# A graph attention kernel: bound of |t| from the norm of the attention vector, transposes on two banks, ten weight halves split inside the attention loop

## What is computed

```python
h = relu(layernorm(x))
HW = h @ W
s, t = HW @ a[:512], HW @ a[512:]
e = leaky_relu(s[row] + t[col], 0.2)
att = softmax of e over the edges of each row
agg = segment_sum(att * h[col], row)
x = x + silu(agg) @ base_w.T + einsum('nip,oip->no', b_splines(agg), spline_w)
h = relu(layernorm(x))
x = x + three graph convolutions of h with batch norm and relu
```

## Time and profile before

| | us |
|---|---|
| median of 3 runs | 684.33 (682.5 to 684.81) |
| the profiled execution | 683.7 |
| its span in the trace | 681.9 |
| TensorE matmuls busy | 604.3 |
| VectorE busy | 477.9 |
| ScalarE busy | 371.5 |
| mean granted TensorE clock | 0.95 of 2.4 GHz |

### The profile page before, as it was taken

The page is one execution under the profiler, slowest core; times in us unless marked ns, Lnnn a source line. Parts: engine busy times, 40 slices in busy tenths (PEclk is TensorE's granted clock), DMA queues, the critical chain, the costliest instruction groups (busy, mean ns, idle before and its releaser), DMA issues.

```text
span 681.9 us, 8727 instructions
## 1 busy us (share of the span) xinstructions
PE 604.3 (89%) x3437; PEld 428.2 (63%) x3437; DVE 477.9 (70%) x739; ACT 371.5 (54%) x486; POOL 23.3 (3%) x30
## 2 busy tenths in 40 slices
PE   3766655999968999999999999869999999999994
PEld 2535643555534455555555555448999899988994
DVE  7989698999785999997369865784344434542354
ACT  1798597545779998987198620328331422332111
POOL 2000000000000000000000000202300020000000
PEclk9798686999979899999999999979999999999998
DMA  8553400000040000000001000090100000001202
GB/s 278 192 186 126 195 1 0 1 1 1 0 151 0 2 1 0 1 1 1 1 1 62 1 0 1 23 369 15 62 1 1 0 1 1 1 0 56 94 38 113
DMA packets 11417, 33.73 MB, mean 49 GB/s; under 512 B 718, under 2 KB 1038, under 8 KB 11120
## 3 DMA queue, kind: packets, MB, share of 16 engines
q1 hardware_dynamic: 11376, 33.17, 13.8%
HBM read 24.78 MB, written 8.40 MB: 49 GB/s over the span
## 4 chain that ended last, share of the span: by engine, by line
PE 67%; DVE 18%; ACT 8%; issue 4%; DVEq 1%; ACTq 1%; DMA 0%; SPq 0%
PE bank L1482 32%; PE bank L1557 20%; PE bank L1526 12%; DVE AL L994 2%; DVE OR L847 2%; DVE OM L850 2%; DVE EX L987 1%; DVE EX L999 1%; DVE SCR L958 1%; ACT CT L599 1%; PE bank L1328 1%; ACT JSQ L532 1%; ACT WKh L606 1%; DVE RDN L1029 1%; DVE hL L1004 1%
## 5 line engine op out<-in xcount | busy, mean ns | idle before, releaser
L1482 PE MATMUL bank<-BHL,WKh 128*128 128x418 f16 x1152 | 207.1, 342 | 4.2 <-DVE BHL L1083 4.2
L1482 PEld LDWEIGHTS bank<-BHL,WKh 128*128 128x128 f16 x1152 | 112.0, 97 | 99.3 <-DVE BHL L1083 4.6
L1557 PE MATMUL bank<-CF,YL 128*128 128x418 f32 x360 | 127.5, 354 | 0.0
L1557 PE MATMUL bank<-CF,YH 128*128 128x418 f32 x360 | 126.6, 352 | 0.0
L1277 DVE TENSOR_TENSOR Z<-bank,dvb 128x418 f32<-128x418 f32 x36 | 21.3, 593 | 69.1 <-PE bank L1557 69.1
L1557 PEld LDWEIGHTS bank<-CF,YL 128*128 128x128 f32 x360 | 67.6, 188 | 1.8
L1557 PEld LDWEIGHTS bank<-CF,YH 128*128 128x128 f32 x360 | 67.7, 188 | 1.0
L784 ACT ACTIVATE bnc<-bnm,tiny 128x1 f32<-128x1 f32 x12 | 3.5, 294 | 104.9 <-DVE bnm L1283 104.9
L1335 PE MATMUL bank<-OM,OR 128*128 128x160 f16 x320 | 32.3, 268 | 19.7 <-DVE OM L850 13.7
L1228 DVE SCALAR_TENSOR_TENSOR YL<-bank,dvc,YH 128x512 fp32r<-128x512 f32 x30 | 21.9, 748 | 38.5 <-ACT YH L765 38.5
L1526 PE MATMUL bank<-GWH,XH 128*128 128x512 f32 x120 | 48.1, 401 | 0.0
(11 more groups left out here) (202 smaller groups left out, 1010.6 us busy)
## 6 DMA issues: line engine op xcount, KB each, us to landing
WKf<-in_wk SPq DMA_DIRECT2D x9, 1024.0 KB, 5.4
c_scratch<-C SPq DMA_DIRECT2D x1, 3200.0 KB, 10.9
GWf<-in_gwT SPq DMA_DIRECT2D x3, 1024.0 KB, 5.4
C<-c_scratch SPq DMA_DIRECT2D x1, 2880.0 KB, 10.4
XT<-in_xT SPq DMA_DIRECT2D x1, 2500.0 KB, 8.8
x_scratch<-XT SPq DMA_DIRECT2D x1, 2500.0 KB, 16.1
XR<-x_scratch SPq DMA_DIRECT2D x1, 2500.0 KB, 8.9
outT<-Z SPq DMA_DIRECT2D x4, 625.0 KB, 3.1
```

The source lines that it names most:

```text
L1482: ins = mm(bank[:, 4 * (g % 2) + o, 0:G], lhs, rhs, start=(u == 0 and q == 0 and i == 0), stop=(u == UNITS - 1 and q == PAIR - 1 and i == 2))
L1557: ins = mm(bank[:, YB + u % YB, 0:G], Y[:, j, o * P:(o + 1) * P], CF[:, j, g * G:(g + 1) * G], start=(j == 0 and i == 0), stop=(j == NT - ...
```

## The change

- ScalarE no longer copies the spread vectors to WAB; VectorE reads them in banks 6 and 7. ScalarE instead takes the squared norm of the vector for t, and from it the bound of |t| (Square and Sqrt, at group 12 of the counts).
- The bound is added to the column of t before TensorE spreads it. The masks' maxima read the spread row in its banks. The reduction for max|t| and the tile U go. Six mask tiles take the place of two, and the scratch of the maxima is f16 in two buffers.
- TensorE transposes tile 0, spreads t, forms the degrees, and then transposes tiles 1 to 9, now with two banks for all. ScalarE does sums of squares 3 and 4 behind tile 0, and 5 to 8 in steps 1, 3, 5 and 7 of the loop. The Exp table is loaded ahead of the first row copies.
- The banks of the attention's sums are dealt out anew, with the denominator last in the first seven tiles. The scale of the weights is formed at step 13, and the second group waits for it.
- The first ten weight halves are split in steps 16 to 25 of the loop: the high half behind the rounding copy of the step on ScalarE, the low half at the end of the step on VectorE. The stretch behind the loop no longer has them.
- Masks and low halves of h are on VectorE, as before.

```diff
+LATE_SQUARES = (1, 3, 5, 7)
 LASTS = 3
+MASKS = 6
+BOUND = 1.02
+FIRST_HALF = 16
...
-        U = at("U", Z4 + 7680, [NP], F32)
-        SCR = at("SCR", Z4 + 8960, [NP], F32)
-        MSK = at("MSK", Z4 + 10240, [2, NP], F16)
-        WAB = at("WAB", Z4 + 12800, [2, D], F32)
+        MSK = at("MSK", Z4 + 5120, [MASKS, NP], F16)
+        JHs = [at("JH0", Z4 + 8960, [NT, D], F16), at("JH1", Z4 + 2560, [NT, D], F16)]
+        SCR = at("SCR", Z4 + 8960, [2, NP], F16)
...
+        def low_weights(g):
+
+            return AL0 if g == 0 else AL12[:, g - 1, :, :]
+
+        def att_bank(g, k):
+
+            return (3, 4, 0)[g] if k == 0 else 4 * ((g + 1) % 2) + k - 1
...
                 if n == 12:
                     act.wait_ge(wa_spread, 1)
-                    nc.scalar.copy(WAB[:, :, :], bank[:, 6:8, :]).then_inc(wa_set, 1)
+                    nc.scalar.activation(JST[:, 0, :], bank[:, 7, :], ACT.Square, accum_out=tb[:, 0:1])
+                    act.drain()
+                    nc.scalar.activation(tb[:, 1:2], tb[:, 0:1], ACT.Sqrt, bias=tiny[:, 0:1], scale=BOUND * D
+                                         ).then_inc(t_bound, 1)
...
-                    nc.scalar.copy(CT[:, t, 5 * b * P:5 * (b + 1) * P], bank16[:, 4 + 2 * (t % 2) + b, 0:5 * P]
+                    nc.scalar.copy(CT[:, t, 5 * b * P:5 * (b + 1) * P], bank16[:, 4 + b, 0:5 * P]
                                    ).then_inc(tposed_out, 1)
 
-            for t in range(5):
-                transposed(t)
+            transposed(0)
+            sum_squares(3, JSQ)
+            sum_squares(4, JSQ)
             act.wait_ge(degs_done, 1)
             nc.scalar.activation(dvc[:, :], bank[:, 3, 0:NT], ACT.Sqrt, bias=1.0).then_inc(degs_out, 1)
-            act.wait_ge(t_spread, 1)
-            act.wait_ge(t_scale, 1)
-            nc.scalar.activation(U[:, :], bank[:, 0:3, :].rearrange("p b c -> p (b c)")[:, 0:NP], ACT.Identity,
-                                 bias=tb[:, 1:2]).then_inc(t_used, 1)
-            for t in range(5, NT):
+            act.wait_ge(squares, 5)
+            for t in range(1, NT):
...
-            sum_squares(3, JSQ2)
-            sum_squares(4, JSQ2)
+            nc.scalar.activation(mv[:, 0, 0:1], tiny[:, 0:1], ACT.Exp)
+            attention_rows(0)
             act.wait_ge(dv_spread, 1)
-            nc.scalar.copy(dvb[:, :], bank[:, 0:3, :].rearrange("p b c -> p (b c)")[:, 0:NP]).then_inc(dvb_set, 1)
-            attention_rows(0)
-            sum_squares(5, JSQ2)
-            sum_squares(6, JSQ2)
+            nc.scalar.copy(dvb[:, :], bank[:, 3:6, :].rearrange("p b c -> p (b c)")[:, 0:NP]).then_inc(dvb_set, 1)
             attention_rows(1)
-            sum_squares(7, JSQ2)
-            sum_squares(8, JSQ2)
-            nc.scalar.activation(mv[:, 0, 0:1], tiny[:, 0:1], ACT.Exp)
-            attention_rows(2)
 
             def exponentials(n):
...
+            def weights_high(u):
+                act.wait_ge(wscale_set, 1)
+                act.wait_ge(agg_unit, DC + 1)
+                if u >= 2:
+                    act.wait_ge(wk_low, u - 1)
+                nc.scalar.mul(weights(u)[:, 0, :], raw_weights(u), wsc[:, 0:1]).then_inc(wk_high, 1)
+
             exponentials(0)
+            attention_rows(2)
             for n in range(NG * NT):
                 g, j = divmod(n, NT)
                 if n + 1 < NG * NT:
                     exponentials(n + 1)
                 act.wait_ge(att_f32, n + 1)
                 nc.scalar.copy(CT[:, j, g * G:(g + 1) * G], EX[:, n % 3, :]).then_inc(att_high, 1)
-
-            def weights_high(u):
-                act.wait_ge(wscale_set, 1)
-                act.wait_ge(att_low, NG * NT)
-                if u >= 2:
-                    act.wait_ge(wk_low, u - 1)
-                nc.scalar.mul(weights(u)[:, 0, :], raw_weights(u), wsc[:, 0:1]).then_inc(wk_high, 1)
+                if n in LATE_SQUARES:
+                    sum_squares(5 + LATE_SQUARES.index(n), JSQ3)
+                if FIRST_HALF <= n < FIRST_HALF + LATE:
+                    weights_high(n - FIRST_HALF)
...
-            weights_high(0)
-            weights_high(1)
             silu_high(0, 0)
-            weights_high(2)
             silu_of(0, 1)
-            weights_high(3)
             silu_high(0, 1)
-            weights_high(4)
             silu_of(1, 0)
-            weights_high(5)
             silu_high(1, 0)
-            weights_high(6)
             silu_of(1, 1)
-            weights_high(7)
             silu_high(1, 1)
             act.wait_ge(agg_unit, (DC + 1) * NG)
-            act.wait_ge(agg_out, DC)
             middle(0)
             middle(1)
             nearest(0)
             nearest(1)
             clipped(0)
-            weights_high(8)
-            weights_high(9)
...
-            dve.wait_ge(wa_set, 1)
+            dve.wait_ge(wa_spread, 1)
             dve.drain()
 
             def projections(k, t0, t1):
                 for t in range(t0, t1):
                     dve.wait_ge(h_rows, t + 1)
-                    V.tensor_tensor_reduce(out=JH[:, t, :], in0=hx[:, t, :], in1=WAB[:, k, :], scale=1.0, scalar=0.0,
+                    V.tensor_tensor_reduce(out=JHs[k][:, t, :], in0=hx[:, t, :], in1=bank[:, 6 + k, :], scale=1.0, scalar=0.0,
                                            op0=ALU.mult, op1=ALU.add, accum_out=st[:, k, t:t + 1])
                 dve.drain()
 
             projections(1, 0, NT)
-            V.tensor_scalar(mx[:, 5, :], st[:, 1, :], LEAK, None, ALU.mult).then_inc(t_cols, 1)
+            dve.wait_ge(t_bound, 1)
+            V.tensor_scalar(mx[:, 3, :], st[:, 1, :], tb[:, 1:2], None, ALU.add).then_inc(t_cols, 1)
+            V.tensor_scalar(mx[:, 5, :], st[:, 1, :], LEAK, None, ALU.mult)
             dve.drain()
             V.tensor_tensor(mx[:, 4, :], st[:, 1, :], mx[:, 5, :], ALU.subtract)
-            projections(0, 0, 6)
-
+            dve.wait_ge(sub_counted, GROUPS)
+            projections(0, 0, NT)
+            V.tensor_scalar(mx[:, 1, :], st[:, 0, :], tb[:, 1:2], None, ALU.subtract)
             dve.wait_ge(t_spread, 1)
             trow = bank[:, 0:3, :].rearrange("p b c -> p (b c)")[:, 0:NP]
-            V.tensor_reduce(tb[:, 0:1], trow, AX, ALU.max, apply_absolute_value=True)
-            dve.drain()
-            V.tensor_scalar(tb[:, 1:2], tb[:, 0:1], 2.0, 1e-30, ALU.mult, ALU.add).then_inc(t_scale, 1)
-            projections(0, 6, NT)
-            V.tensor_scalar(mx[:, 1, :], st[:, 0, :], tb[:, 1:2], None, ALU.subtract)
-            dve.wait_ge(degs_out, 1)
-            V.reciprocal(dvc[:, :], dvc[:, :]).then_inc(dvc_set, 1)
-            dve.wait_ge(t_used, 1)
-            dve.wait_ge(sub_copied, GROUPS)
 
             def mask(s):
-                if s >= 2:
-                    dve.wait_ge(masked, s - 1)
-                V.tensor_scalar(MSK[:, s % 2, :], C16[:, s, :], 1.0, None, ALU.min).then_inc(mask_set, 1)
+                if s >= MASKS:
+                    dve.wait_ge(masked, s - MASKS + 1)
+                V.tensor_scalar(MSK[:, s % MASKS, :], C16[:, s, :], 1.0, None, ALU.min).then_inc(mask_set, 1)
...
-                else:
-                    dve.wait_ge(masked, s)
+                if s >= 2:
+                    dve.wait_ge(masked, s - 1)
                 dve.wait_ge(mask_set, s + 1)
-                V.tensor_tensor_reduce(out=SCR[:, :], in0=MSK[:, s % 2, :], in1=U[:, :], scale=1.0, scalar=0.0,
+                V.tensor_tensor_reduce(out=SCR[:, s % 2, :], in0=MSK[:, s % MASKS, :], in1=trow, scale=1.0, scalar=0.0,
                                        op0=ALU.mult, op1=ALU.max, accum_out=mx[:, 0, s:s + 1]).then_inc(masked, 1)
...
+            dve.wait_ge(sub_copied, GROUPS)
             mask(0)
             for i in range(NG):
                 for t in range(*SETS[i]):
                     largest(t)
                 columns(i)
+                if i == 0:
+                    dve.wait_ge(degs_out, 1)
+                    V.reciprocal(dvc[:, :], dvc[:, :]).then_inc(dvc_set, 1)
...
-                if n == 3:
-                    dve.wait_ge(squares, KB)
-                    V.tensor_reduce(wsc[:, 0:1], wss[:, :], AX, ALU.add).then_inc(sumsq_set, 1)
                 if n >= 1:
                     attention_low(n - 1)
                 attention_f32(n)
                 if n == 9:
+                    dve.wait_ge(squares, KB)
+                    V.tensor_reduce(wsc[:, 0:1], wss[:, :], AX, ALU.add).then_inc(sumsq_set, 1)
+                if n == 13:
                     weight_scale()
-                if n == 12:
+                if n == 14:
                     denominators(0)
                     aggregated(0, 0)
-                if n == 13:
+                if n == 15:
                     aggregated(0, 1)
                     aggregated(0, 2)
-                if n == 14:
+                if n == 16:
                     aggregated(0, 3)
-                if n == 23:
+                if FIRST_HALF <= n < FIRST_HALF + LATE:
```

(90 more changed lines are left out.)

17 lines of the change are left out of this document (8 added, 9 removed).

## The result

| | before | after |
|---|---|---|
| median of 4 runs each, us | 684.08 (682.5 to 684.81) | 692.11 (691.11 to 693.16) |
| profiled execution, us | 683.7 | 692.22 |
| its span, us | 681.9 | 690.4 |
| first low half of the attention weights | 115.38 | 105.35 |
| last low half | 180.01 | 198.94 |

The changed kernel takes 1.0121 times the time of the one before, 95% interval 1.0097 to 1.0144: some 8 us slower. Everything happened ahead of the first turn unit. The front gave 10.0 us, the loop took 29.0, the stretch behind it gave 10.0.

A forecast was written before the change was run, and what follows sets the result against it. TensorE bounds from 223 us, so time moves with the first turn unit (turn 0's spline matmuls); before it, waits between engines decide. -9.0 + 28.3 + 1.0 - 10.7 = +9.6 on 683.7: 693.3, stated as 693.5, range 688.5 to 698.5.

The forecast's parts named there:

- The closed circle: Loop steps 16 to 25: VectorE and ScalarE wait for each other at each weight split, 4.53 us a step, +28.3.
- Rival (a): Loop: the splits really hide, each costing VectorE only its 1.20; turn unit at 216.4, -6.7, 677 us; 8%.
- The front: Up to the attention weights' first low half: without the |t| reduction and VectorE's wait, 106.4 instead of 115.38, gain 9.0.
- The t spread: Front, TensorE: the 20 matmuls that spread t take 0.13 each, 2.5 us.
- The first pair: Front, TensorE: the first pair of row spreads, after the transposes, takes 2.0 us.
- The meeting point: End of the front: TensorE and VectorE meet, the third pair of row spreads starting at about 101.4 (before: 109.07).
- Two banks: Front: transposing 18 half tiles with two banks instead of four takes 0.75 us per half tile, 13.5 us.
- Reads from banks at nothing: Front, VectorE: operations reading banks in place of SBUF cost nothing more; bounds 0 and 2.4 us.
- Squares: Loop steps 1, 3, 5 and 7: four sums of squares on ScalarE delay the next copies, +1.0, between 0 and 2.
- The stall of 2.99 us in the degrees: Front, TensorE: a stand with no releaser; returning later it would cost up to 2.6 us, taken as 0.
- The tail: From the last low half to the first turn unit: 32.4 us instead of 43.1, -10.7.
- Rival (b): Loop: TensorE, starved, falls to its lower clock; turn unit at 237.6, +14.5, 698 us; 8%.

The follow-up runs named there:

- Experiment 1: The changed kernel with the low half of each weight piece formed one step later on VectorE than its high half on ScalarE: 675.01 us.
- experiment 2: The changed kernel with its ten weight halves split behind the loop again, all other parts of the change kept: 677.73 us.
- experiment 3: The changed kernel without the four sums of squares in the loop, the weight scale formed from five of nine sums: one run, 690.7 us.
- experiment 4: The changed kernel with seven weight halves in the loop, low halves one step late, and three behind it in gaps of the Silu chain: 672.52 us.
- experiment 6: experiment 4 with the weight scale one step and the first group's divisions up to two steps earlier: 672.19 us.
- experiment 8: experiment 6 with the low half of weight half 8 moved behind the third Silu's low half on VectorE, half 9's behind the fourth's: 670.44 us.
- experiment 9: experiment 8 with the third group's denominators behind all Silu low halves, half 8's low half between the third and fourth, half 9's last: 667.9 us.
- experiment 5: The changed kernel with four banks instead of two for the transposes of tiles 1 to 9: 691.16 us.
- experiment 7: experiment 6 with the four transpose banks of experiment 5: 672.33 us.

## Why the prediction was right, and where its terms were off

693.5 was forecast, slower with a chance of 0.89; 692.11 was measured, inside the range of 688.5 to 698.5.

- **The closed circle** (+28.3 for ten steps, 4.53 each): 4.51 to 4.52 measured, VectorE idle 1.66 where 1.7 stood. The plain step of 1.70 was read at one of the last two steps, 178.31 to 180.01, which have no sum and a wait of 0.60 for the copy in its place; that it is as long as the steps with a sum (159.63 to 161.34) is luck. Experiment 1 opens the circle alone and takes 17 us away. Rival (a) had the price of a split that hides nearly right (1.20, measured 1.07 once the circle is open, and 675 us where it said 677); the order of the queues kept it from coming true, as the text said.
- **The front** (-9.0): -10.0 in this execution. In the traces of experiments 1 to 4, 6, 8 and 9, which have the same front, the first low half lies between 103.5 and 105.9, so -9.5 to -11.9: the forecast was a little too small in all of them. The masks began 0.7 late (80.52 for 79.8; 0.6 of it was that the projections began at 67.34 and not 66.77), and the stretch of maxima was 0.8 shorter than before, since from one maximum to the next it is 1.81 (81.32 to 83.13) where it was 1.94; the scratch has two buffers and is f16, and six masks stand ready, and which of these gives the 0.13 no run separates. The t spread was mis-sized: 2.5 was taken from 0.13 per matmul, it took 4.64, at a granted clock of 0.50 from 73 to 80 us; the kernel before had needed 3.27 for the same 20. The first pair was mis-sized too (2.0 taken, 3.10 measured), and the second and third the other way (2.9 taken, 1.50 and 1.57 measured). All these prices were copied from other stretches, and the granted clock moves between them (below); their errors cancel in part, which is luck. The meeting point, 101.4 forecast, was 101.87.
- **Two banks** (0.75 per half tile): 0.75. Experiments 5 and 7 show that it bounds nothing by more than a microsecond.
- **Reads from banks at nothing**: right, by the maxima (1.48 from banks, 1.49 from SBUF, though their output became f16 as well) and by the projections (0.68 to 0.69 on both sides, with only the source changed). By the estimate from the Trainium skill (VectorE: DVE Perf Modes, section on the TRN2 errata) the 30 instructions would have cost 1.9 us more; this trace does not show them.
- **Squares** (+1.0): 0.9 by experiment 3. The stall of 2.99 us in the degrees, taken at 0, did not come.
- **The tail** (-10.7, 32.4): -10.0, 33.07. A Silu with rounding and low half takes 2.9 (200.42 to 203.28) and not 2.7: the Silu itself 0.80 to 0.91, and a small handover after each part. The TensorE gap of 8 was 8.0.
- **Rival (b)**, the lower clock in the starved loop: the granted clock from 145 to 193 us was 0.89, TensorE caught up with its operands each time, and nothing came of it.

The loop grew by 29.0, of which experiment 3 gives 0.9 to the squares and so 28.1 to the ten splits. The sum of the measured terms is -10.0 + 28.1 + 0.9 - 10.0 = +9.0; the first turn unit moved by 8.9. The prediction's sum, +9.6, was near it partly because the front's and the tail's misses (1.0 and 0.7) had opposite signs.

What the prediction priced too low is the clock behind TensorE's gap. It took 0.1795 per matmul as the pace of the turn units; that is the mean of a piece that begins slowly. In the kernel before, the granted clock in the 8 us from 223 is 0.66, in the 8 us from 232 of the changed one 0.73. Both kernels have a gap (4.2 us before, 8.0 after), so the difference between them held (458.8 us from the first turn unit to the end, and 458.4); but a version that closes it gains what no term of the sum contained.

What stays open: which of three causes makes VectorE wait 4.56 us in experiment 2, and why the front sometimes runs at a higher granted clock. Between 80 and 106 us it was 0.68 in the changed kernel and 0.92 in experiment 1, with pairs of half tiles every 1.50 and 1.24 us; the low half of step 0 lies up to 2.4 us apart from one execution to another.

## What to carry to other kernels

Before work is put into the gaps of a loop, write down who waits for whom inside one step: if the helper engine makes its part and the main engine uses it in the same step, both idle in turn and the parts add up; one step of delay (two lines changed, no buffer more) turned a loss of 1.2% into a gain of 1.4%. Behind a loop, order each engine's list by the chain that others wait on: moving 1.2 us of work that nobody wanted yet towards the end of VectorE's list was worth 1.3 us by the trace, and moving 3.4 us more was worth 2.5 us by the medians. And where the matmul engine stands idle ahead of its longest stretch, the gap costs its length and then the slow start, so it does less harm where other work hides both.

## What the runs showed of the hardware

- Behind a gap in TensorE's work (4.16 us before, 7.95 in the changed kernel, 6.77 in experiment 8), the first 7 to 8 us of the turn units had a mean granted clock of 0.66, 0.73 and 0.65, so part of them ran at 1.2 GHz; without a gap (experiment 9) it was 1.00, all at 2.4 GHz. The difference is some 2 us on 1104 matmuls. The Trainium skill (TensorE: Matmul & The Clock Gate, What's actually happening) calls the halved clock of 1.2 GHz the default that activity lifts; the traces agree.
- A custom reduction of VectorE with its second source in banks takes as long as one with both in SBUF: over 512 elements 0.68 to 0.69 us and 0.69, over 1280 elements 1.48 (f16 out) and 1.49 (f32 out).
- The same transposes and spreads run at different clocks: between 80 and 106 us the granted clock was 0.68 in the changed kernel and 0.92 in experiment 1, and the same 12 matmuls of 128 columns took 1.57 us in the changed kernel and 2.93 in the one before.
